# A state-space block in which VectorE rotates the next step's product ahead of the current step's low parts

## What is computed

```python
def apply_ssm(Lbar_r, Lbar_i, B_bar_r, B_bar_i, C_real, C_imag, D, x):
    Bu_r = jnp.einsum('blh,ph->blp', x, B_bar_r)
    Bu_i = jnp.einsum('blh,ph->blp', x, B_bar_i)
    A_r = jnp.broadcast_to(Lbar_r, Bu_r.shape)
    A_i = jnp.broadcast_to(Lbar_i, Bu_i.shape)
    _, _, xs_r, xs_i = jax.lax.associative_scan(binop, (A_r, A_i, Bu_r, Bu_i), axis=1)
    ys = jnp.einsum('blp,hp->blh', xs_r, C_real) - jnp.einsum('blp,hp->blh', xs_i, C_imag)
    return ys + D * x
...
y_f = s5(fwd_..., x)
y_b = s5(bwd_..., x_flip)
return y_f + jnp.flip(y_b, axis=1)      # s5 is discretize, apply_ssm, gelu
```

## Time and profile before

| | before |
|---|---|
| median of 3 runs | 737.09 us (737.0 to 737.13) |
| profiled execution, its own time | 737.35 us |
| its span, first to last instruction | 735.3 us |
| mean granted TensorE clock | 0.94 |
| busy over the span: PE | 658.3 us (90%) |
| DVE | 532.1 us (72%) |
| POOL | 422.9 us (58%) |
| ACT | 260.1 us (35%) |

### The profile page before, as it was taken

One profiled execution on the slowest core, in us unless ns is written; L12 is line 12 of the kernel. 1 busy time (PEld: TensorE's weight loads), 2 busy tenths in 40 slices (PEclk: granted clock), 3 DMA queues, 4 the chain that ended last, 5 costly groups with the idle time before them and its releaser, 6 DMA issues. The chain is left out here.

```text
span 735.3 us, 11947 instructions
## 1 busy us (share of the span) xinstructions
PE 658.3 (90%) x3277; PEld 489.4 (67%) x3277; DVE 532.1 (72%) x1139; ACT 260.1 (35%) x514; POOL 422.9 (58%) x727
## 2 busy tenths in 40 slices
PE   0799999949958999999799589999999999999995
PEld 0577777727646878787576367777777777777772
DVE  7688888853976788878439757777777777777774
ACT  2222223124631222222256434444444434443440
POOL 1789999110540433333515437777777777777774
PEclk9999999966968999999979689999999999999997
DMA  6200000000000000000000000000000000000000
GB/s 233 44 1 0 1 1 0 0 0 1 0 1 0 1 0 1 0 0 1 0 1 0 2 0 15 15 14 15 14 14 14 14 14 14 14 14 14 14 15 15
DMA packets 12918, 9.58 MB, mean 13 GB/s; under 512 B 4316, under 2 KB 12636, under 8 KB 12636
## 3 DMA queue, kind: packets, MB, share of 16 engines
q1 hardware_dynamic: 12876, 9.27, 4.0%
q10 hardware_dynamic: 16, 0.00, 0.0%
HBM read 5.07 MB, written 4.20 MB: 13 GB/s over the span
## 5 line engine op out<-in xcount | busy, mean ns | idle before, releaser
L1352 PE MATMUL ex_pE<-WdP,ex_hid 128*128 128x512 f32 x774 | 190.8, 401 | 0.0
L1352 PEld LDWEIGHTS ex_pE<-WdP,ex_hid 128*128 128x128 f32 x774 | 139.8, 187 | 42.4 <-issue 6.8
L1549 POOL TENSOR_TENSOR ex_s<-ex_ms 128x256 f32<-128x256 f32 x129 | 94.9, 735 | 72.0 <-DVE ex_ms L1518 66.9
L1518 DVE TENSOR_TENSOR ex_ms<-ex_pE,ex_gl 128x512 f32<-128x512 f32 x128 | 88.1, 689 | 62.0 <-POOL ex_picked L1553 56.4
L723 DVE TENSOR_TENSOR inv_prod<-inv_pW,m_img 128x504 f32<-128x504 f32 x144 | 91.7, 681 | 18.0 <-PE inv_pW L638 16.3
L1209 POOL TENSOR_TENSOR hT<-hT,ssm_gelu 128x512 f32<-128x512 f32 x32 | 47.7, 1509 | 94.6 <-ACT ssm_gelu L1182 94.6
L1551 POOL TENSOR_TENSOR ex_s<-ex_s 128x128 f32<-128x128 f32 x129 | 91.4, 709 | 10.1
L649 PE MATMUL inv_pS<-ident,inv_prod 128*128 128x128 f32 x576 | 88.3, 276 | 5.6 <-DVE inv_prod L723 4.9
L649 PEld LDWEIGHTS inv_pS<-ident,inv_prod 128*128 128x128 f32 x576 | 70.5, 141 | 28.5 <-DVE inv_prod L723 20.2
L800 POOL TENSOR_TENSOR u<-ln_u,u 128x512 fp32r<-128x512 f32 x28 | 37.2, 1351 | 72.1 <-ACT u L869 72.1
L638 PE MATMUL inv_pW<-inv_ysb,m_conv2L 98*128 98x512 f32 x144 | 69.9, 488 | 2.3 <-DVE inv_ysb L711 2.3
(11 more groups left out here) (232 smaller groups left out, 1086.4 us busy)
## 6 DMA issues: line engine op xcount, KB each, us to landing
m_img<-in_x SPq DMA_DIRECT2D x2, 2048.0 KB, 9.0
out<-ex_res SPq DMA_DIRECT2D x16, 256.0 KB, 2.3
WdT<-in_L_ffn_Wd SPq DMA_DIRECT2D x2, 256.0 KB
W1z<-in_L_ffn_W SPq DMA_DIRECT2D x2, 64.0 KB
bd<-in_L_ffn_bd SPq DMA_DIRECT2D x4, 2.0 KB
m_Bm<-in_L_attn_fwd_B_real SPq DMA_DIRECT2D x2, 16.0 KB, 2.0
m_Bm<-in_L_attn_fwd_B_imag SPq DMA_DIRECT2D x2, 16.0 KB, 2.1
m_Bm<-in_L_attn_bwd_B_real SPq DMA_DIRECT2D x2, 16.0 KB, 2.0
```

The costliest lines, as they stand in the source:

```text
L1352: last = nc.tensor.matmul(o, hid[par][value][:, h, start:start + P], g.WdP[weight][:, h], start=(h == 0 and (value, weight) == PARTS[0]), ...
L1518: nc.vector.tensor_tensor(ms[j % 2][:], pE[BANK[par][j]][:], gl[:, 4, j, :].unsqueeze(2).broadcast_to([128, EX, F]), ALU.mult).then_inc(ch ...
L1549: nc.gpsimd.tensor_tensor(s4[slot][0:P], m[:, 0:4], m[:, 4:8], ALU.add).then_inc(pl, 1)
```

## The change

`step` loses its rotation to a function of its own, `rotate`. The first rotation is issued ahead of the first step. Each step then consists of its scan, its back-rotation, the rotation of the next step with its wait for `entered`, the wait for the high parts and the low parts. The last step of the last batch has no next rotation, so the last batch is written out instead of being the loop's last pass. TensorE, ScalarE and GpSimd are not touched.

```diff
-                def step(b, s, n0):
+                def table(s):
                     d, h = ORDER[s]
+                    return [g.tab[:, d, k, h * CH:(h + 1) * CH] for k in range(2)]
+
+                def rotate(b, s):
                     n = b * STEPS + s
-                    r, zz = rot[s % 2], z[s % 2]
-                    cos, sin = (g.tab[:, d, k, h * CH:(h + 1) * CH] for k in range(2))
+                    d, _ = ORDER[s]
+                    r, (cos, sin) = rot[s % 2], table(s)
                     v.wait_ge(entered, n + 1)
                     nc.vector.tensor_tensor(r[:, 0, :], scan_order(pV[s % 2][0][:], d), cos, ALU.mult)
                     nc.vector.tensor_tensor(r[:, 1, :], scan_order(pV[s % 2][1][:], d), sin, ALU.mult).then_inc(freed, 1)
                     v.wait_ge(freed, n + 1)
                     nc.vector.tensor_tensor(r[:, 0, :], r[:, 0, :], r[:, 1, :], ALU.add).then_inc(turned, 1)
+
+                def step(b, s, n0, more):
+                    d, h = ORDER[s]
+                    n = b * STEPS + s
+                    r, zz, (cos, sin) = rot[s % 2], z[s % 2], table(s)
                     v.wait_ge(turned, n + 1)
...
                     nc.vector.tensor_tensor(back[0][:], zz[:], cos, ALU.mult)
                     nc.vector.tensor_tensor(back[1][:], zz[:], sin, ALU.mult).then_inc(backed, 1)
+                    if s + 1 < STEPS:
+                        rotate(b, s + 1)
+                    elif more:
+                        rotate(b + 1, 0)
                     v.wait_ge(highs, n + 1)
...
+                rotate(0, 0)
                 for s in range(STEPS):
-                    step(0, s, True)
-                with v.Fori(1, B) as b:
+                    step(0, s, True, True)
+                with v.Fori(1, B - 1) as b:
                     for s in range(STEPS):
-                        step(b, s, False)
+                        step(b, s, False, True)
+                for s in range(STEPS):
+                    step(B - 1, s, False, False)
```

## The result

| | before | after |
|---|---|---|
| median | 737.11 us (737.0 to 737.36, 4 runs) | 773.32 us (769.79 to 775.1, 4 runs) |
| ratio, 95% interval | | 1.0485 (1.0447 to 1.0522) |
| profiled execution | 737.35 us, span 735.3 | 769.79 us, span 767.8 |
| mean granted clock | 0.940 | 0.946 |

The change makes the kernel 4.9% slower, 36.2 us.

What follows compares the result with a forecast made beforehand. TensorE sets the pace, VectorE close behind; the change closes a loop between their in-order queues. Loop +30.76 and first step +0.64 give 31.4, clock falls 9.2: 40.6 on 737.09 gives 777.7, predicted 778, range 769 to 790.

Steps and rivals of the forecast that it cites:

- The loop: State space: low parts release TensorE's N product, then next V product, rotation, next low parts, without overlap; 43.10 us per batch.
- T: T(n) is when TensorE starts the first N product of step n; 4.29 us to the next V product, forward step.
- enter: TensorE's V product for a step, start to end of its last matmul: 2.96 us when plain.
- rotation to low parts: VectorE, from the start of the next step's rotation to the start of the low parts: 1.92 us.
- The intervals without a fall: Time between first N products of successive steps, at full TensorE clock: forward 10.56, backward first 10.66, backward second 11.32 us.
- The last one: Interval from T(14) to T(15), which has no rotation in it: 6.20 us.
- the sum: T(0) to T(15) without the clock: 156.62 us against 125.86 before, +30.76.
- The first step: Rotation of step 1 goes into VectorE's 1.2 us wait for the high parts; T(0) moves by +0.64 us.
- GpSimd: Its additions no longer meet VectorE's low parts, which take 1.30 us; rival that they still meet: 793, chance 0.05.
- The clock: TensorE's waits lower its clock: 6 falls at 1.54, 9.2 us; rivals 0 or 1 (0.13), 11 to 15 (0.10).
- The 5: Clock falls assumed among the 14 TensorE waits after the first, bounds 0 and 14.
- the stand of 2.92 us: TensorE's wait ahead of T(15) before the change; it left the clock at 1.00, so 5 was put below half.

Runs made afterwards that it cites:

- The first experiment: Changed kernel with TensorE's V products issued one step earlier, VectorE's new order kept: 729.29 us beside 734.42 for the kernel before, ratio 0.9929.
- the third: Kernel in which only the second step of each batch has the next rotation ahead of the low parts: 753.43 us beside 734.42 before, ratio 1.0245.
- the fourth: Changed kernel with six more KI matmuls, results overwritten, ahead of each TensorE wait for the low parts: 766.37 us, ratio 1.0470.
- the second trace of before: Kernel before, run again unchanged for another trace: 735.96 us (729.02 to 737.32).
- the two kernels with the earlier V product: V products one step earlier on TensorE, with VectorE's new order (729.29 us) and with its old order (731.10 us, ratio 0.9971).
- the additional multiplications in the kernel before: Kernel before with four unused 512-column VectorE multiplications per step between back-rotation and next rotation: 765.45 us beside 736.54.

## Why the prediction came out right

**The loop.** Each term was met. T to the next enter 4.29 us (predicted 4.29), enter 2.95 (2.96), rotation to low parts 1.93 (1.92), low parts 1.29 (1.30). The intervals without a fall are 10.56, 10.56, 10.64 and 11.31 us (10.56, 10.56, 10.66, 11.32). The last one would have been 395.91 - 389.80 = 6.11 by VectorE's chain (6.20), and was 6.55 because TensorE was late there. The first experiment opens the loop and the whole loss is gone; the third closes it once per batch and pays its share; the fourth has 156.7 us where the sum had 156.62.

**The first step.** T(0) moved from 232.56 to 233.25: +0.69, predicted +0.64, and TensorE's stand there grew from 3.67 to 4.30. The timeline of after, which answers the earlier trace rows, shows the rotation going into the wait for the high parts at no price but these tenths:

```profile
229.38 0.69 DVE L1149 TENSOR_TENSOR ssm_back<-ssm_z,tab 128x512 f32<-128x512 f32 x1
229.98 0.68 DVE L1131 TENSOR_TENSOR ssm_rot<-ssm_v,tab 128x512 f32<-128x512 f32 x1
...
231.91 1.29 DVE L1156 TENSOR_TENSOR ssm_z<-ssm_back,ssm_z 128x512 fp32r<-128x512 f32 x2
...
233.25 2.29 PE L1079 MATMUL ssm_y<-ssm_z,N 128*128 128x512 f32 x6 [4.30 <-DVE ssm_z L1156]
```

**GpSimd.** Its pair ended at 296.77, half a us ahead of the rotation and 2.4 us ahead of the low parts at 299.19, where I had 1.9. The low parts take 1.29 in 15 steps and 2.38 in the last, where there is no rotation to hold them back.

**The clock.** This is the term that was mis-sized. I had six falls at 1.54, 9.2 us. Between T(0) and T(15) four intervals are longer by a fall: 12.11 twice for 10.56, 12.87 for 11.31, 12.20 for 10.64, 1.55 us each, 6.2 in all. A fifth fall lies between T(14) and T(15). There TensorE would have stood for the low parts, so only the part of the fall beyond that stand counts, 396.35 - 395.91 = 0.44 us. Together the falls cost 6.6 us where I had 9.2. The price of a fall behind a wait was right, and "after T a fall counts in full" fails for the last one. What was off is the count: one and four falls instead of one and five, the last of the four almost hidden. The 5 was a choice between 0 and 14, so that it came this close is luck. My argument from the stand of 2.92 us was weak as well: the second trace of before shows a fall behind the very same stand.

**What I did not have at all.** T(15) moved by 396.35 - 358.42 = 37.9 us, the span by 32.5. The 5.4 us between them lie behind T(15), where the program is the same. The first row below is before, the second after, both from about 5.6 us behind T(15) to where the experts are under way:

```profile
364.00:420.00 56.00, 44.98 (x231) 32.26 (x232) 37.04 (x87) 29.48 (x60) 24.60 (x24) 0.80 0.00 0
```

```profile
402.00:453.00 51.00, 40.00 (x230) 28.74 (x231) 36.53 (x87) 29.15 (x60) 24.41 (x23) 0.89 0.00 1
```

TensorE does all but the same work, 231 and 230 instructions, in 56 and in 51 us, at a granted clock of 0.80 and of 0.89. From the layer norm's first matmul (L843) to the experts' first, TensorE takes 419.36 - 364.65 = 54.7 us before and 452.62 - 402.46 = 50.2 us after: 4.5 of the 5.4 us. The change is not needed for such a difference. The same stretch takes 51.1 us in the second trace of the kernel before, 50.2 again in that of the changed one, 54.7 in the kernel with the stands filled, 54.7 and 51.1 in the two kernels with the earlier V product, and over all the traces from 50.2 to 57.4. The code of this stretch is the same in all of them, so several us of a total depend on how the clock falls there. What decides it stays open. The other three timed executions of the changed kernel, 772.88 to 775.1 us, had a mean clock of 0.934 to 0.939 against 0.946, so they probably paid what the traced one saved; no trace of them exists.

So in the traces 31.4 us of loop and first step, met to a few tenths, and 6.6 of clock give the 37.9 by which T(15) moved, and 5.4 of clock elsewhere, which I had set to zero, bring the span to 32.5. The medians differ by 36.2, my forecast by 40.6. Both errors of the clock made the time shorter than forecast, and the two medians of this kernel, 773.32 and 769.53, both lie inside 769 to 790, the second one only just. The mechanism was right, and that the total stayed in range owes something to luck. The 0.2% that I said a measurement can tell was too fine as well: it came from three runs on one chip, and on the chips of the experiments the kernel before spreads by 11 us.

## What to carry to other kernels

Before moving an instruction with a wait ahead of another one on the same queue, write down who produces what it waits for and what that producer waits for in turn. If the way leads back to the instruction that was passed, a loop through two in-order queues closes, and each turn costs the sum of its members, however idle the engines look. Such a reordering comes in a pair with the producer's: here issuing the V product one step earlier on TensorE turned +4.9% into -0.7% against the kernel before.

## What the runs showed of the hardware

Two low parts take three different times, by how many of the two start while one of GpSimd's additions is running. One low part alone takes 0.69 us, one that starts during an addition 1.75 to 1.82 us. None is met where GpSimd is idle: the pair takes 1.29 us. In the steady step before the change GpSimd starts between them and only the second is met: 2.39. Where GpSimd is just ahead of the first and its second addition follows at once, both are met: 3.5. The kernel with the earlier V product shows the last four steps in a row, with GpSimd ahead by 0.02 to 0.10 us:

```profile
235.81 2.99 POOL L1225 TENSOR_TENSOR hT<-hT,ssm_gelu 128x512 f32<-128x512 f32 x2 [16.07 <-ACT ssm_gelu L1198]
...
235.83 3.52 DVE L1157 TENSOR_TENSOR ssm_z<-ssm_back,ssm_z 128x512 fp32r<-128x512 f32 x2
```

Being first is not the whole of it. In the step behind these four GpSimd is again ahead by 0.09 us, but its second addition comes only at 270.00, and the pair takes 2.38:

```profile
267.32 2.38 DVE L1157 TENSOR_TENSOR ssm_z<-ssm_back,ssm_z 128x512 fp32r<-128x512 f32 x2
```

It isn't always VectorE that pays. With the additional multiplications in the kernel before, three of the 16 steps had the low parts at 1.29 us and GpSimd's pair at 4.2 to 4.3 instead of 2.53. In the one shown, GpSimd's first addition took 3.02 us instead of 1.29, while three VectorE instructions with two inputs in SBUF, a multiplication and the two low parts, followed one another without a gap from 344.82 to 346.72:

```profile
344.85 4.27 POOL L1212 TENSOR_TENSOR hT<-hT,ssm_gelu 128x512 f32<-128x512 f32 x2 [6.96 <-ACT ssm_gelu L1185]
...
345.43 1.29 DVE L1147 TENSOR_TENSOR ssm_z<-ssm_back,ssm_z 128x512 fp32r<-128x512 f32 x2
```

Other VectorE instructions with two inputs in SBUF are hit too. In the kernel with the earlier V product the scan took 2.32 us at 300.55 instead of 1.22, and 14 of the 32 multiplications of the back-rotation 1.5 to 1.8 us instead of 0.69, so GpSimd's price had partly moved from the low parts to them. The rotation's two products, which read one operand from PSUM, took 0.67 to 0.69 us in every step of every trace:

```profile
L1132 DVE TENSOR_TENSOR ssm_rot<-ssm_v,tab x16: 676/684/692, 223.7 to 338.3; 128x512 f32<-128x512 f32 x16
...
L1150 DVE TENSOR_TENSOR ssm_back<-ssm_z,tab x16: 679/686/1792, 227.7 to 345.5; 128x512 f32<-128x512 f32 x16
```

These lines give shortest, middle and longest in ns. This goes with what the Trainium skill ("SBUF — State Buffer", SBUF: two separate sides) says: whichever starts first holds the shared ports for its whole instruction, and the other one waits.

Stands of TensorE of 1.8 to 2.6 us, repeated every 10.6 us, brought the clock to its lower level four times in 15 intervals, beside the fall behind the first stand of 4.30; stands of at most 1.21 us in their place, and 2.90 once at the start, brought none. The length of a stand alone doesn't tell: the stand of 2.92 us before the change was followed by a fall in one trace and not in the other, and in the kernel before with the four multiplications eight stands of 1.5 to 2.5 us ahead of T(2) to T(10) went with a single fall, at 284 to 292 us.
